# A decoder layer's expert stage: the dense batch's groups moved among the further expert tiles, the shared expert moved behind the last tile

## The reference, cut to what matters

```python
shared_out = silu(x @ shared_gate_w) * (x @ shared_up_w) @ shared_down_w
probs = softmax(x @ gate_w)
topk_w, topk_idx = lax.top_k(probs, 8)          # 64 experts, 8 chosen for each token
topk_w = topk_w / topk_w.sum(-1, keepdims=True)
for e in range(64):                             # c = combine weight of expert e
    out += c[:, None] * ((silu(x @ gw[e]) * (x @ uw[e])) @ dw[e])
out += sigmoid(x @ shared_expert_gate_w) * shared_out
```

## Time and profile before

| | us |
|---|---|
| median of 3 runs | 1000.52 (996.49 to 1005.32) |
| the profiled execution, as timed | 995.45 |
| its span in the profile | 993.6 |
| mean granted clock of TensorE | 0.907 of full |

### The profile page before, as it was taken

How to read it: one execution, slowest core, us unless ns; L and a number is a source line. 1 busy time by engine, 2 the same in 40 slices (tenths; PEclk the granted TensorE clock), 3 DMA queues, 4 the chain that set the end, 5 groups by cost and what they waited for, 6 DMA issues and landing times.

```text
span 993.6 us, 19997 instructions
## 1 busy us (share of the span) xinstructions
PE 859.9 (87%) x6286; PEld 672.2 (68%) x6317; DVE 620.6 (62%) x1794; ACT 520.9 (52%) x1114; POOL 564.4 (57%) x752
## 2 busy tenths in 40 slices
PE   5987999999999999898887866499998896689897
PEld 3766777777777777565554544379997795479554
DVE  6747778777887786887776643733443452245466
ACT  2424677667666766565554443557764452235221
POOL 3695757665767862005665455564973456444660
PEclk9987999999999999999898777559999997779799
DMA  6200212222122112576675433658776796578630
GB/s 155 61 21 17 70 50 84 73 61 83 55 82 71 48 44 65 139 195 206 198 217 184 149 129 132 221 176 252 238 221 201 223 291 203 154 213 285 193 105 21
DMA packets 126035, 138.74 MB, mean 140 GB/s; under 512 B 25318, under 2 KB 111910, under 8 KB 125934
## 3 DMA queue, kind: packets, MB, share of 16 engines
q1 hardware_dynamic: 89390, 81.89, 28.9%
q0 software_dynamic: 11520, 31.47, 10.2%
q10 hardware_dynamic: 25024, 24.12, 7.6%
HBM read 76.44 MB, written 60.83 MB: 138 GB/s over the span
## 4 chain that ended last, share of the span: by engine, by line
PE 32%; another core or an unknown queue 8%; DVE 7%; POOL 6%; issue 4%; ACT 4%; DMA 1%; SPq 1%; ACTq 0%; DVEq 0%; POOLq 0%
PE bank L2386 5%; PE bank L2411 5%; PE bank L2365 3%; PE bank L1531 2%; PE bank L2207 2%; DVE xmax L1541 2%; PE bank L1608 2%; POOL got_rows L2596 2%; PE bank L1633 2%; POOL got_rows L2597 2%; PE bank L2187 1%; POOL got_rows L2595 1%; PE bank L2392 1%; PE bank L2383 1%
## 5 line engine op out<-in xcount | busy, mean ns | idle before, releaser
L2610 POOL DMA_INDIRECT got_rows<-ys,slot_idx x120 | 115.9, 966 | 110.7 <-issue 33.0
L1856 POOL DMA_INDIRECT xs<-xrow,slot_idx x120 | 116.2, 968 | 83.7 <-issue 31.9
L964 ACT ACTIVATE probs<-bank 128x512 f32<-128x512 f32 x192 | 113.9, 604 | 85.1 <-PE bank L776 48.1
L1708 ACT ACTIVATE probs<-bank 128x512 f32<-128x512 f32 x128 | 74.7, 597 | 91.1 <-PE bank L1608 45.8
L1541 DVE TENSOR_REDUCE xmax<-bank 128x2 f32<-128x512 f32 x128 | 86.1, 685 | 43.2 <-remote 21.9
L2518 DVE TENSOR_TENSOR xrow<-owner,bank 128x256 f32<-128x256 f32 x60 | 25.2, 420 | 104.7 <-issue 65.9
L774 PE MATMUL bank<-query,keys 128*128 128x256 f32 x256 | 82.6, 346 | 0.5 <-ACT probs L964 0.4
L1087 DVE TENSOR_REDUCE blockmax<-bank 128x32 f32<-128x512 f32 x96 | 63.1, 687 | 26.7 <-PE bank L726 25.5
L1608 PE MATMUL bank<-query_x,keys_x 114*128 114x512 f32 x128 | 66.1, 521 | 9.6 <-issue 4.1
L1531 PE MATMUL bank<-keys_x,query_x 112*128 112x256 f32 x256 | 61.2, 327 | 5.5 <-DVE xmax L1541 4.6
L1531 PEld LDWEIGHTS bank<-keys_x,query_x 112*128 112x128 f32 x256 | 49.5, 213 | 19.3 <-DVE xmax L1541 10.3
(11 more groups left out here) (404 smaller groups left out, 2516.8 us busy)
## 6 DMA issues: line engine op xcount, KB each, us to landing
ys<-y_tile ACTq DMA_DIRECT2D x62, 256.0 KB
xs<-zero_b SPq DMA_DIRECT2D x16, 512.0 KB, 3.2
up_res<-in_w_up SPq DMA_DIRECT2D x16, 512.0 KB
ys<-xn ACTq DMA_DIRECT2D x30, 256.0 KB
keys_x<-key_rows_x SPq DMA_DIRECT2D x32, 192.0 KB
ctx_in<-in_ctx SPq DMA_DIRECT2D x32, 128.0 KB, 2.5
key_rows_x<-ctx_hi SPq DMA_DIRECT2D x256, 16.0 KB, 1.5
query_x<-xq_rows_hi SPq DMA_DIRECT2D x64, 64.0 KB
```

Of the source, the lines that this page charges most:

```text
L964: nc.scalar.activation(probs[:, u, :], SCORE[u % 2][:], ACT.Exp, scale=SCALE)\
L1708: nc.scalar.activation(probs4[b % 2][:, u, :], XSCORE[n % 2][:], ACT.Exp, scale=XSCALE)\
L1856: nc.gpsimd.indirect_dma_start(out=xs, out_offset=bass.IndirectOffsetOnAxis(ap=slot_idx[:, r, k:k + 1], axis=0), in_=xrow[r % XROW_RING], ...
L2610: nc.gpsimd.indirect_dma_start(out=got_rows[:, g % GOT_RING, :], out_offset=None, in_=ys[0:T * (E + 8 * r + 8), :], in_offset=bass.Indirec ...
```

## The change

- **Dense groups.** Each of the 16 groups now stands inside the tile loops, at pairs 34, 37, 41, 45, 49, 53, 56, 60, 64, 68, 72, 75, 79, 83, 87 and 91 (`dense_pair`): its up matmuls at the end of PE's step p, its transposes at the end of step p+1, its down matmuls at the end of step p+2. All three use one bank (5). Gate, hidden and transposed values have one buffer each. The down result no longer adds up in PSUM: each group has its own `dense_add` on DVE, so 16 adds instead of one, and a group's up matmuls wait for the add of the group before.
- **Rings.** The up results have three banks instead of four, `hid_s` and `hid_t` two buffers instead of three. The transposes of hidden values stand at the end of step p for pair p-3 instead of inside it for p-4, the down matmuls at p-5 instead of p-6, and ACT's copy and store follow one step earlier.
- **Shared expert.** All four groups stand behind the last tile. Nothing of it is left between routing and the first tile on PE, and DVE's part stands among the tiles (j = 66 to 76).
- **Combining.** 8 combines to every 9 tiles instead of 11 (from 88 as before), so about 88 of the 120 stand inside the loop instead of about 73. The adds of the shared expert stand behind combines 90, 92, up to 104.

```diff
-HIDDEN_AT, ADD_AT, DENSE_AT = 76, 62, 78
+HIDDEN_AT, ADD_AT, DENSE_AT = 66, 90, 50
...
-        hid_s = [xrow_all[:, n, :] for n in range(3)]
-        hid_t = [owner[:, 6:8, :], xrow_all[:, 3, :].rearrange("p (a t) -> p a t", a=2), hid_pairs[:, 2]]
-        TURN_BANK, UP_BANK, DOWN_BANK = bank[0:2], bank[2:6], bank[6:8]
-        HID_BANK = [UP_BANK[n][:, 256:512] for n in range(4)]
+        hid_s = [xrow_all[:, 2 + n, :] for n in range(2)]
+        hid_t = [owner[:, 6:8, :], hid_pairs[:, 2]]
+        TURN_BANK, UP_BANK, DOWN_BANK, DENSE_BANK = bank[0:2], bank[2:5], bank[6:8], bank[5]
+        HID_BANK = [UP_BANK[n][:, 256:512] for n in range(3)]
         FIRST, TILE_PAIRS = E // 2, TILES // 2
+        dense_pair = [FIRST + 2 + (TILE_PAIRS - 3 - FIRST) * n // (GROUPS - 1) for n in range(GROUPS)]
...
-            for n in range(EARLY):
-                shared_keep(act, n)
...
+        SHARED_Y = [bank[k] for k in (2, 3, 6, 7, 4, 5, 2, 3)]
+        hidden_sh = [tile[0:I].rearrange("p a d -> p (a d)").bitcast(F32) for tile in x_tile]
+        dense_gate, dense_hid, dense_hidT = owner[:, 0:2, :], owner[:, 2:4, :], xrow[0]
...
         def dense_up(pe, n):
-            if n == 0:
-                pe.wait_ge(S("tile_y"), ended("tile_y") + TILES)
-            if n >= 2:
-                pe.wait_ge(S("dense_read"), n - 1)
+            if n:
+                pe.wait_ge(S("dense_added"), n)
...
         def dense_silu(act, n):
             act.wait_ge(S("dense_up"), n + 1)
-            if n >= 2:
-                act.wait_ge(S("dense_read"), n - 1)
...
         def dense_turn(pe, n):
             pe.wait_ge(S("dense_weighed"), n + 1)
-            if n == 0:
-                pe.wait_ge(S("sharedT_kept"), ended("sharedT_kept") + 4)
-            if n >= 2:
-                pe.wait_ge(S("dense_kept"), n - 1)
             for a in range(2):
-                last = nc.tensor.transpose(DENSE_T[n % 2][:, 128 * a:128 * a + 128], dense_hid[n % 2][:, a, :], ident[:])
+                last = nc.tensor.transpose(DENSE_BANK[:, 128 * a:128 * a + 128], dense_hid[:, a, :], ident[:])
...
         def dense_down(pe, n):
             pe.wait_ge(S("dense_kept"), n + 1)
-            if n == 0:
-                pe.wait_ge(S("shared_added"), ended("shared_added") + 5)
             for a in range(2):
                 q = 2 * n + a
-                last = nc.tensor.matmul(DENSE_Y[:, 0:D], dense_hidT[n % 2][:, 128 * a:128 * a + 128],
-                                        down_res[:, D * q:D * q + D], start=q == 0, stop=q == E // 2 - 1)
+                last = nc.tensor.matmul(DENSE_BANK[:, D:2 * D], dense_hidT[:, 128 * a:128 * a + 128],
+                                        down_res[:, D * q:D * q + D], start=a == 0, stop=a == 1)
             last.then_inc(S("dense_down"), 1)
 
-        def dense_add(dve):
-            dve.wait_ge(S("dense_down"), GROUPS)
-            dve.wait_ge(S("shared_added"), ended("shared_added") + B // 2)
-            nc.vector.tensor_tensor(X[:, NS, :], X[:, NS, :], DENSE_Y[:, 0:D], ALU.add).then_inc(S("dense_added"), 1)
+        def dense_add(dve, n):
+            dve.wait_ge(S("dense_down"), n + 1)
+            if n:
+                dve.wait_ge(S("dense_added"), n)
+            nc.vector.tensor_tensor(X[:, NS, :], X[:, NS, :], DENSE_BANK[:, D:2 * D], ALU.add).then_inc(S("dense_added"), 1)
...
             def up_pair(p):
                 pe.wait_ge(S("tile_kept"), ended("tile_kept") + 2 * p + 2)
-                if p in (2, 3):
-                    pe.wait_ge(S("shared_added"), ended("shared_added") + p + 3)
-                if 4 <= p < FIRST + 4:
-                    pe.wait_ge(S("tile_hidden"), ended("tile_hidden") + 2 * p - 6)
-                elif p >= FIRST + 4:
-                    pe.wait_ge(S("tile_hidT"), ended("tile_hidT") + 2 * (p - FIRST) - 6)
+                if 3 <= p < FIRST + 3:
+                    pe.wait_ge(S("tile_hidden"), ended("tile_hidden") + 2 * p - 4)
+                elif p >= FIRST + 3:
+                    pe.wait_ge(S("tile_hidT"), ended("tile_hidT") + 2 * (p - FIRST) - 4)
                 for r in range(2):
-                    out = UP_BANK[p % 4][:, 128 * r:128 * r + 128]
+                    out = UP_BANK[p % 3][:, 128 * r:128 * r + 128]
...
             odd_spread(pe)
-            shared_turn(pe, 0)
-            shared_turn(pe, 1)
-            shared_down(pe, 0)
-            shared_turn(pe, 2)
-            shared_down(pe, 1)
-            shared_down(pe, 2)
+            pe.wait_ge(S("logits_kept"), B)
             pe.wait_ge(S("slots_ready"), ended("slots_ready") + NS)
-            pe.wait_ge(S("shared_added"), ended("shared_added") + 2)
+            pe.wait_ge(S("xpv_kept"), B)
+            pe.wait_ge(S("rows_turned"), 1)
             pe.wait_ge(S("sides_swapped"), 6)
             pe.wait_ge(S("ld_down_res"), ended("ld_down_res") + 16 * 8)
-            for p in range(TILE_PAIRS + 6):
+            for p in range(TILE_PAIRS + 5):
                 if 0 <= p - 2 < TILE_PAIRS:
                     up_pair(p - 2)
                 if p - 1 < TILE_PAIRS:
                     values(p - 1)
-                if FIRST <= p - 4 < TILE_PAIRS:
-                    turn_hidden(p - 4)
                 if p < TILE_PAIRS:
                     turn_pair(p)
                 if 0 <= p - 4 < FIRST:
                     down_pair(p - 4)
-                if FIRST <= p - 6:
-                    down_pair(p - 6)
-            shared_turn(pe, EARLY)
-            shared_down(pe, EARLY)
-            for n in range(GROUPS + 2):
-                if n < GROUPS:
-                    dense_up(pe, n)
-                if 0 <= n - 1 < GROUPS:
-                    dense_turn(pe, n - 1)
-                if 0 <= n - 2:
-                    dense_down(pe, n - 2)
+                if FIRST <= p - 5:
+                    down_pair(p - 5)
+                if FIRST <= p - 3 < TILE_PAIRS:
+                    turn_hidden(p - 3)
+                for n, at in enumerate(dense_pair):
+                    if p == at:
+                        dense_up(pe, n)
+                    if p == at + 1:
+                        dense_turn(pe, n)
+                    if p == at + 2:
+                        dense_down(pe, n)
+            shared_turn(pe, 0)
+            for n in range(B // 4):
+                if n + 1 < B // 4:
+                    shared_turn(pe, n + 1)
+                shared_down(pe, n)
...
+                for n, at in enumerate(dense_pair):
+                    if p == at:
+                        dense_silu(act, n)
+                    if p == at + 1:
+                        dense_keep(act, n)
+            for n in range(B // 4):
+                shared_keep(act, n)
...
             for j in range(1, TILES + 4):
                 if j % 2 == 1:
+                    if FIRST <= j // 2 - 2 < TILE_PAIRS:
+                        hidden_turned(j // 2 - 2)
                     if j < TILES:
                         hidden_pair(j // 2)
-                    if FIRST <= j // 2 - 2 < TILE_PAIRS:
-                        hidden_turned(j // 2 - 2)
+                    for n, at in enumerate(dense_pair):
+                        if j // 2 == at - 1:
+                            dense_hidden(dve, n)
+                        if j // 2 == at + 1:
+                            dense_add(dve, n)
                 if j == ROWS_AT:
                     combine_rows(dve)
                 if j > ROWS_AT and (j - ROWS_AT) % WEIGH_GAP == 0 and (j - ROWS_AT) // WEIGH_GAP <= 8:
                     combine_reduce(dve, (j - ROWS_AT) // WEIGH_GAP - 1)
                 if j == ROWS_AT + 8 * WEIGH_GAP + 1:
                     combine_scale(dve)
-                if j == HIDDEN_AT:
-                    shared_gates(dve, 1)
-                if j == HIDDEN_AT + 4:
-                    shared_hidden(dve, EARLY)
-                if j == HIDDEN_AT + 20:
+                if j in (HIDDEN_AT, HIDDEN_AT + 1):
+                    shared_gates(dve, j - HIDDEN_AT)
+                if j in range(HIDDEN_AT + 4, HIDDEN_AT + 12, 2):
+                    shared_hidden(dve, (j - HIDDEN_AT - 4) // 2)
+                if j == DENSE_AT:
                     dense_weights(dve)
-                while g < 8 * NS and COMBINE_AT + 11 * g // 8 <= j:
+                while g < 8 * NS and COMBINE_AT + 9 * g // 8 <= j:
                     combine(dve, g)
                     g += 1
             for g in range(g, 8 * NS):
                 combine(dve, g)
-                if g >= DENSE_AT and (g - DENSE_AT) % 2 == 0 and (g - DENSE_AT) // 2 < GROUPS:
-                    dense_hidden(dve, (g - DENSE_AT) // 2)
-                if g >= ADD_AT and (g - ADD_AT) % 2 == 0 and 2 * EARLY <= (g - ADD_AT) // 2 < B // 2:
+                if g >= ADD_AT and (g - ADD_AT) % 2 == 0 and (g - ADD_AT) // 2 < B // 2:
                     shared_add(dve, (g - ADD_AT) // 2, g + 1)
-            dense_add(dve)
```

(34 more changed lines are left out.)

83 lines of the change are left out of this document (34 added, 49 removed).

## The result

The changed kernel takes 1025.45 us (median; 1017.63 to 1026.23), against 1002.92 for the kernel before in the same set of runs (996.49 to 1015.30). The ratio is 1.022, with a 95% interval from 1.012 to 1.032: slower by over 1%. A fourth execution took 1967.63 us at a granted clock of 1.00; nothing explains it, and of the figures here only the median counts it. The forecast was 1032 with a range of 975 to 1056. The profiled execution has a span of 1022.8 us (forecast 1024.8) and a mean clock of 0.908, as before 0.907.

The account below looks back on a forecast made before the run. PE sets the time in dense groups; late signals during gather bursts stop the tiles. -8 + 44.8 - 64.1 + 32.1 = +4.8, plus 26.4 of losses, takes 993.6 to 1024.8 us, 1032 as a median; range 975 to 1056.

Parts of the forecast that it names:

- front: Before the tiles: the three shared groups go away, so the start moves 8 us earlier (between 0 and 8.9).
- 16 groups with their waits: In the tile loop: 16 dense groups at 2.80 us of PE's time, 44.8 us, plus 8 us of waits.
- more loss: In the tile loop: gather batches, moved by POOL catching up, stop the tiles more, +18.4 us without the groups' waits.
- tail: From the last tile's down matmuls to the span's end: 64.1 us become 32.1 (bounds 22.2 and 32.1).
- (a): Two of the last three gather batches, formerly beside the tail, now fall in the tile loop: 2 x 5.8 = +11.6 us.
- (c): In the tile loop: the long run of gathers that lost 22.2 us becomes two ordinary bursts, -10.6 us.
- (b): In the tile loop: six gather batches formerly free of loss may each cost 5.8 us; half taken, +17.4 (0 to +34.8).
- Signals arriving late while POOL issues a batch without pause: Tile loop: this reading, not full DMA engines, explains the stopped tiles; ordinary losing stretches cost 5.8 us.
- Shallower rings: In the tile loop: an undisturbed pass fits under a step of 2.41 us, so fewer banks and buffers add 0.
- Losses shrink: Rival, tile loop: the loss is transfers queueing in the DMA engines and shrinks; middle 979 us, chance 0.26.
- Losses as before: Rival, tile loop: only a long run of gathers hurts, bursts beside dense matmuls stay free; +2.2 us, 1003, chance 0.17.
- The rings decide: Rival, tile loop: signals later than the rings' slack cost their excess every step; +30 us, 1062, chance 0.11.

Follow-up runs that it names:

- e6: The kernel before, unaltered, run again for a trace in a late set: 988.39 us.
- e5: The changed kernel, unaltered, run again in a late set: 1019.65 us, ratio 1.0225 to the kernel before.
- quiet: The one set of runs (e1 to e4) where the kernel before took 921 us and no trace has a wait put down to "remote".
- e4: The kernel before with each of the 120 gathers replaced by a POOL memset, quiet set: 913.04 us.
- e1: The changed kernel with each of the 120 gathers replaced by a POOL memset, quiet set: 938.15 us.
- late: The sets of e5 to e12, where the kernel before took 988 to 1005 us and "remote" waits are frequent, as in the first pair of traces.
- e3: The changed kernel with each batch's gathers opened two by two, nothing left out, quiet set: 938.51 us.
- e8: The changed kernel without the dense batch's sixteen groups, late set: ratio 0.989 to the kernel before.
- e11: The changed kernel with each batch's gathers opened two by two, late set: 980.08 us, ratio 0.988 to the kernel before.
- e12: The changed kernel with each gather replaced by a POOL memset, late set: 963.00 us, ratio 0.972 to the kernel before.
- e10: The changed kernel with gathers of 64 bytes instead of 1 KB a row, late set: 1043.12 us, ratio 1.038 to the kernel before.
- e2: The changed kernel with gathers of 64 bytes instead of 1 KB a row, quiet set: 934.79 us.
- e9: The kernel before with only the changed kernel's shallower rings, late set: ratio 1.009 to the kernel before.

## Why the prediction held, and by how much each term was off

The kernel became slower for the reason forecast, in the stretch forecast: the groups enter a loop that PE sets, the tail gives back less, and bursts of gathers cost more. That the spans agree within 2 us is partly luck. The medians differ by 22.5 us, where the spans of the two profiled executions differ by 29.2, and below single terms miss by up to 17 us and cancel.

The sum by its terms, in us. The second pair is e6 and e5, the quiet one e4 and e1. Losses are what a loop takes beyond 147.5 (before) and 200.7 (after). The 53.2 is the difference of these two, measured in the quiet set and put into the late columns; it holds the rings too:

| | forecast | first traces | second pair | quiet |
|---|---|---|---|---|
| front | -8 | -5.0 | -1.3 | -1.4 |
| 16 groups with their waits | +52.8 | +53.2 | +53.2 | +53.2 |
| more loss | +18.4 | +13.2 | +27.2 | 0 |
| tail | -32.0 | -32.2 | -49.4 | -27.5 |
| sum of spans | +31.2 | +29.2 | +29.7 | +24.3 |

**Loss before.** 45.5 us were read from stretches; against a loop without gathers it is 196.0 - 147.5 = 48.5. The undisturbed step of 2.41 holds: 60 of them make 144.6 of the 147.5. The loss is not waiting alone. The loop of the kernel after, and of e3, which loses nothing (columns as in the stretches above):

```profile
728.50:990.90 262.40, 216.97 (x1243) 177.98 (x1242) 112.74 (x278) 94.88 (x213) 109.01 (x111) 0.92 0.57 170
```

```profile
704.00:904.70 200.70, 196.32 (x1243) 164.48 (x1242) 111.90 (x278) 99.06 (x212) 108.82 (x109) 1.00 0.73 221
```

PE's busy time for the same 1243 records grows by 20.7 us, at a mean granted clock of 0.92 instead of 1.00. So a third of the 61.7 us is matmuls at a lower clock in stretches where PE had paused, and two thirds are pauses. The forecast had both in its 5.8 us a batch.

**Front.** The direction was right and the size 3 us too large. The 3.2 us for a load in the prediction are read from a wrong row: `xs<-zero_b` in the earlier trace rows is the writing of zeros, 512 KB each. The value does no harm: in the kernel after the first load is issued at 648.8, and the transposes that wait for it start at 651.8. The fourth pair's transposes did come 9.9 us earlier (657.34 against 667.27), even above my bound of 8.9, since its load was issued 4.9 us earlier than I had taken for fixed. But by the first further pair only 5.0 are left: PE waits 2.6 us for the next load there, and its clock is 0.97 on average in 656 to 728.5, where it was 1.00 after 667 before, 2 of 72.5 us. The bound looked at one pair and not at what the gain becomes on its way. In the quiet set nearly nothing is won: in e1 the first pair waits 12.6 us for its load, which waits for POOL's scatters, and in e4 the shared groups lie under that same wait (first transposes at 627.4 and 628.1).

**Groups.** 2.80 and 0.5 each, 52.8 in all, against 53.2, which also holds what the rings cost in a quiet set. Late runs give 22 to 45 us for the groups alone (e8), so for them the term was too large. Of it PE's wait for DVE's weighting is 3.8 us in 16 times, 0.24 each, half of what I took. The 27.1 us of after looked like a mis-sized term, but with late signals this is where the burst's loss shows, as e11 (7.2) and e12 (3.8) tell.

**Moved past POOL.** The gathers came in batches of 8 opened by landings, 12.8 to 20.2 us apart, though not "without pause": POOL's 28 runs of 4.3 show that it often waited for its own landings. Thirteen batches lost 61.7 us, 4.7 each, against 5.8 in the forecast. (a) and (c) came true: no four pairs of the loop have more than 9 gathers beside them, where before two stretches had 16 and 11. (b), half of the loss for the six free batches, was a guess that came out about right: two batches stayed nearly free (0.6 us around 791.5 to 804.3 and 1.0 around 857 to 871). Why these are free was not found.

**Reading of the mechanism.** "Signals arriving late while POOL issues a batch without pause" was called no proof. It now stands on e10 (bytes gone, loss stays), e12 (gathers gone, loss goes) and e11 (pauses added, two thirds of the loss goes). What the reading lacked is that only PE's signals are late: every "remote" wait of all late traces ends with one. Nor are gathers enough, since in the quiet set e2 has runs of 6 gathers on average and no such wait. How PE's signal comes to be late (in PE, on the way, or in its record) is not shown by any run.

**Shallower rings.** Taken at 0; measured at 4 to 14 us where signals are late (e9). The rival's "+30 in every step" did not come, since the signals in the loop are late only beside POOL's gathers. As part of "more loss" it is in the sum already, so this term was missing, and by luck (b) covered for it.

**Tail.** 31.9 against 32.1, with shared matmuls at 3.09 to 3.78 a group and 8.73 us for the last 15 combines. That the tail of before is anything from 57.0 to 79.1 us, as the signal for its shared group comes in time or not, was not foreseen. In e6 it takes 15.0 us more than in the first trace and the loop 11.5 less: the loss stands at another place, and the sum of the table stays.

**Rivals.** "Losses shrink" is refuted by e10, and the rule it leaned on (the Trainium skill, DMA: Bandwidth & Descriptors, section "SWDGE vs HWDGE vs iDMA") explains none of the loss: software and hardware queues share the engines in e3 too, at a share of 0.73, and the loop there takes 200.7 us. "Losses as before" (+2.2 us) is wrong in both its parts: the losses grew by 13.2 and 27.2 us, and even in the quiet set, without losses on either side, the change costs 24.3 us, where the forecast's terms without more loss make +12.8. The front gave 1.4 instead of 8 and the tail 27.5 instead of 32. So with the losses taken away the forecast's sum would have been 11.5 us short. "The rings decide" missed by its size. Work that PE did at full pace behind the tiles costs it more among them, 53.2 us for a tail that shrinks by 27.5 to 32 (49.4 in the second pair). The tail can't shrink by more, since shared groups, last gathers and last combines need 29 to 32 us there, in which PE is half idle (busy 16.7 of 31.9 us in the kernel after).

**A faster version.** Opening the gathers two by two is 3.4% faster than the changed kernel in late sets (0.988 against 1.022, each to the kernel before beside it). In the quiet set it takes as long as the changed kernel without gathers (938.5 against e1's 938.2). Against the kernel before it is 0.971 to 1.004 in the late set and 1.013 to 1.024 in the quiet one, so it does not beat it for certain, and loses to it in the quiet set. The kernel before with its gathers opened two by two was not run.

## What to carry to other kernels

A move to "fill gaps" pays only by the idle time of the engine that sets the pace: count its busy time in the stretch that the work leaves (41.4 of 42.5 us here) before giving it any gain. Run a kernel once without the suspected cause before you explain a loss by it: the loops of 147.5 and 200.7 us made every later number readable. And where POOL issues indirect DMAs beside a tightly coupled pipeline and the trace shows waits put down to nothing, try pauses between them, bound to the pipeline's own progress, rather than open a batch at once.

## What the runs showed of the hardware that was not expected

- The same kernel on the same chip took 921 us in one set of runs (917 to 927) and 988 in the next (986 to 1016). The traces differ in waits put down to nothing: none in the one, and in the other 63 to 80 us from 460 to 640, beside the scatters, alone.
- In the late sets PE's signals to ACT and DVE are late beside POOL's indirect DMAs, up to 17 us after PE's work ended (913.8 to 931.2 in e6); the longest single wait is 8.2 us (e9). No signal of another engine is among them. Before 400, where POOL issues no indirect DMA, e12 has only 9.1 us of such waits in 16 times. The size of the rows does not matter, 64 bytes or 1 KB.
- In the quiet set 106 gathers of 128 KB beside the tiles cost the pipeline less than 0.1 us (e3 against e1).
